# Attention and mixture-of-experts layer on one core: the order of VectorE in the local attention, the place of the expert loads and splits, and the rope's buffers are changed

## The chip, the cores and the metric

One Trainium2 chip, one of its cores. The metric is the device time of one execution in microseconds; lower is better. The engines are named as the profile names them: PE (TensorE, matmul; PEld its weight loads), DVE (VectorE), ACT (ScalarE), POOL (GpSimd), SP (SyncE, which here only issues DMAs).

## The reference

```python
x  = L0_attn_x                       # (2, 1024, 256), float32
xn = layernorm(x)
return x + attention(xn) + experts(xn)
```

Attention: 16 query heads on 4 key-value heads. Each score is the sum of a "semantic" product (32 wide) and a "geometric" product (32 wide, with rope), scaled, times exp(logit_scale) of the head. The first 896 keys are pooled to 14 block means of 64 keys each; the last 128 keys are kept as they are, so there are 142 keys. A query sees the keys whose position is not after its own. Softmax, weighted values, output projection.

Experts: 16 experts, the top 4 of a softmax over 16 logits per token, weights normalised; each expert is silu(x G) * (x U) and a down projection, 256 to 224 to 256. The reference computes all experts and picks; the kernel computes only the chosen ones.

## The kernel before, in words

The five engines run programs of their own, written out by hand and tied by semaphores. The order in which each engine's instructions are written is the order in which it runs them, so a waiting instruction holds up all behind it. On DVE, `link` makes the engine wait for its own last result (needed when the next instruction reads it).

The work comes in four stages.

1. Layer norm, router, ranking of the tokens by expert, block means of the keys. POOL then writes each token's row to the place of each of its four experts in memory, by indirect DMA (L715): 16 groups of 4, each group waited for (L720-L721) before the next. SP loads experts 0 to 3 early (EARLY = 4).

2. The local part: the last 128 queries of both batches, which see all 142 keys. It has eight units (UNITS: 2 batches x 4 key-value heads). For unit n:
   - PE `l_score` (L1510, two banks; it waits until the exponentials of n-2 have read the banks), DVE `l_largest` (L1177), ACT `l_exp` (L835), DVE `l_probabilities` (reciprocal L1184, L1185, L1187, then semaphore l_p), PE `l_turn` (L1527, waits l_p), ACT `l_keep` (L842), PE `l_value` (L1536, waits for the copy of the values before, l_osb), DVE `l_values` (L1193).
   - PE's loop (L1655-L1661): turn n, score n+2, value n-1, `beside(n)`. DVE's loop (L1241-L1248): probabilities n+1, largest n+2, values n-1, `beside(n)`.
   - `beside` is side work. DVE: at n = 0 `build_values` and `diagonals` (L1142, L1145, L1126; they wait for PE's products of that step), at 2 `keep_tables` (L1205 to L1216), at 3, 4 and 7 `split_low` of an expert's weights (L1197, L1198). PE: at 0 the products for the values, at 1 to 3 `fold_values`, at 1 a spread of the task table, at 5 and 6 `fold_queries`.

3. The block part, `attention` over seven pairs of query tiles t (REMOTE = 7). Each step ropes and projects the queries of t+1 while it scores t and attends t-1. `rope_q` (L1147-L1158) reads the projected queries from a PSUM bank: two sine products to q2, a link, the cosine product in place in the bank, a link, the sum to q1. `probabilities` (L1295-L1306) writes the reciprocals of the sums to PSUM columns and multiplies.
   During this stage SP stores and loads residual tiles (`store_sum` L586, `load_residual` L580) and loads the experts 4 to 15 in the seven lots of LATE = ((4, 5), (6, 7), (8, 9), (10, 11), (12,), (13,), (14, 15)) (`load_late` L591; each expert is three DMAs, L401-L403, of 224 KB each). `load_residual(i)` waits until the store two tiles before has landed; `load_behind` (L618) waits for scores of a pair.
   The weights are used as a high half and a low half. ACT makes the high halves (`split_high`, L817 and L818), in the block part those listed for t in SPLITS (L378), 11 and 12 at the head of stage 4, 13 to 15 in its steps 5 to 7. POOL makes the low halves of experts 4 to 12 (L692, L695): 4 and 5 between its last groups, 6 to 12 in a loop after them. DVE makes those of 0 to 3 and 13 to 15.

4. The experts: 79 tiles of 128 rows, software-pipelined. In `step(j)` (L1716) PE turns the input of tile j+2 (L1723), does gate and up of j+1, turns the activations of j (L1747), does the down projection of j-1: 16 matmul instructions a tile. Gate-up of tile 10 waits until all low halves exist (L1734). ACT copies the result y (L938) to one of four buffers; from the fifth on it waits until the scatter of the buffer's last use has landed. POOL scatters y into the output with an add (L742), and begins only after its low halves, with all residual stores landed (L729-L731). SP may load the first expert inputs when the scores of the last pair are done (L640) and all 16 groups of POOL have landed (L642).

Of the kernel before, what the change touches and what calls it, by code (L numbers as in the profile page):

```python
# [32 lines left out]
ALU = mybir.AluOpType  # L33
# [3 lines left out]
P = 128  # L37
# [55 lines left out]
def build(nc, x, wq_sem, wk_sem, wq_geo, wk_geo, wv, wo, logit_scale, router_w, expert_bias, gate, up, down,  # L93
# [9 lines left out]
    with ctx:  # L103
# [72 lines left out]
        bd_g = wat.take("bd_g", [P, HKV, NB, NBLK, G])  # L176
        pr = [wat.take(f"pr{u}", [P, HK]) for u in range(NB)]
        smax = [wat.take(f"smax{u}", [P, H]) for u in range(NB)]
        ssum = wat.take("ssum", [P, NB, H])

        wl = r_loop[0]
        q2 = wl.take("q2", [P, H * DS])
# [192 lines left out]
        FOLD_BANKS = (4, 4, 4, 0)  # L375
        STARTS_BANK = 1
        HIGH_AT = {0: 0, 1: 1, 5: 2}
        SPLITS = ((), (4, 5), (), (6, 7), (8, 9), (10,), ())  # L378
        HEAD = (11, 12)
        SENT = 11  # L380
        BETWEEN = (4, 5)
# [31 lines left out]
        def turned_bank(u, t):  # L413

            return bank[u + 6 if t.last else u]
# [138 lines left out]
        def _(sp):  # L554
# [25 lines left out]
            def load_residual(i):  # L580
                for u in range(NB):
                    if 0 < i < REMOTE - 1:
                        sp.wait_ge(c_stored[u], i * DMA)
                    sp.dma_start(residual(u, i)[:, :], rows(x_rows, u * TB + i)).then_inc(lx_in if i == REMOTE - 1 else xr_in[i % 2][u], DMA)

            def store_sum(i):  # L586
                for u in range(NB):
                    sp.wait_ge(c_out[u], i + 2)
                    sp.dma_start(rows(out_rows, u * TB + i), residual(u, i)[:, :]).then_inc(c_stored[u], DMA)

            def load_late(i):  # L591
                for k in LATE[i]:
                    load_expert(sp, k, w_late[i])
# [18 lines left out]
            sp.wait_ge(tables_ready, 1)  # L612
            for s in range(TRASH):
                sp.wait_ge(scattered[s], DMA)
            load_residual(1)
            load_late(0)
            load_residual(REMOTE - 1)
            def load_behind(n, t):  # L618

                for u in range(NB):  # L620
                    sp.wait_ge(c_s[u], t)
                load_late(n)

            for i in range(REMOTE - 3):
                store_sum(i)
                load_residual(i + 2)
                if i < 3:
                    load_late(i + 1)
                else:
                    load_behind(4, 2)  # L630
            store_sum(REMOTE - 3)
            load_behind(5, 4)

            def load_task(j, s):
                tile = sp.value_load(td_i[0:1, ds(j, 1)], min_val=0, max_val=N * K // P - 1)
# [310 lines left out]
        def _(dve):  # L946
# [197 lines left out]
                                        pmask.rearrange("p (g n h) -> p g n h", g=1, n=1).to_broadcast([P, HKV, NB * NBLK, 2]), ALU.mult)  # L1144
                nc.vector.tensor_copy(vb[:, :, FOLD - NB:FOLD], rep[:, :, NB * NBLK:XF]).then_inc(vb_built, 1)  # L1145

            def rope_q(raw_bank, u, t, done):  # L1147

                raw = raw_bank[:, :].rearrange("p (g h d) -> p g h d", g=H, h=2)
                t2 = q2[:, :].rearrange("p (g h d) -> p g h d", g=H, h=2)  # L1150
                co = cos[:, ds(t * RH, RH)].rearrange("p (o d) -> p o d", o=1).to_broadcast([P, 2 * H, RH])
                for half in range(2):
                    sn = sin[:, ds(t * DS + half * RH, RH)].rearrange("p (o d) -> p o d", o=1).to_broadcast([P, H, RH])
                    last = nc.vector.tensor_tensor(t2[:, :, half, :], raw[:, :, 1 - half, :], sn, ALU.mult)
                link(last)
                by_half = raw_bank[:, :].rearrange("p (g d) -> p g d", d=RH)
                link(nc.vector.tensor_tensor(by_half, by_half, co, ALU.mult))
                nc.vector.tensor_tensor(q1[u][:, :], raw_bank[:, :], q2[:, :], ALU.add).then_inc(done, 1)  # L1158

            def over_keys(v, n=H, k=NBLK):  # L1160
                return v.rearrange("p (h o) -> p h o", o=1).to_broadcast([P, n, k])
# [1 line left out]
            for u in range(NB):  # L1163
                dve.wait_ge(l_q, u + 1)
                if u:
                    dve.wait_ge(l_rope, u)
                rope_q(bank[L_Q[u]], u, REMOTE, l_rope)
            bound_tasks()

            def l_largest(n):  # L1170
# [66 lines left out]

            l_largest(0)
            l_largest(1)
            l_probabilities(0)  # L1240
            for n in range(UNITS):  # L1241
                if n + 1 < UNITS:
                    l_probabilities(n + 1)
                if n + 2 < UNITS:
                    l_largest(n + 2)
                if n:
                    l_values(n - 1)
                beside(n)  # L1248
# [20 lines left out]
            def rope(u, t):  # L1269

                dve.wait_ge(c_q[u], t.count(1))
                if not t.first:
                    dve.wait_ge(c_qt[u], t.count(0))
                if u or not t.first:
                    dve.wait_ge(c_rope[1 - u], t.count(u))
                rope_q(bank[2 + u], u, t.number, c_rope[u])

            def shifted(u, t):

# [15 lines left out]
            def probabilities(t):  # L1295
                dve.wait_ge(c_sum, 2 * t.number + 2)
                if t.first:

                    link(nc.vector.tensor_scalar(ssum[:, :, :], ssum[:, :, :], more[:, 0:1], None, ALU.add))
                srec = [turned_bank(u, t)[:, 0:H] for u in range(NB)]  # L1300
                for u in range(NB):
                    last = nc.vector.reciprocal(srec[u], ssum[:, u, :])
                last.then_inc(c_rec, 1)
                dve.wait_ge(c_rec, t.count(1))
                for u in range(NB):
                    nc.vector.tensor_tensor(by_key(pr[u], t), by_key(pr[u], t), over_heads(srec[u], t), ALU.mult).then_inc(c_p[u], 1)  # L1306

            def attended(u, t):

# [513 lines left out]
```

## Time and profile before

| what | us |
|---|---|
| median of 3 runs | 394.54 |
| lowest and highest | 391.06, 396.1 |
| the profiled execution | 391.06 |
| its span, first to last instruction | 389.3 |
| PE busy | 348.6 (90%) |
| DVE busy | 238.0 (61%) |
| POOL busy | 230.4 (59%) |
| ACT busy | 183.3 (47%) |
| mean granted clock of TensorE | 0.974 |

The busy times are sums over the span and overlap each other. The span leaves out what lies before the first and behind the last instruction, here 1.8 us. All rows further down are of this one execution, in microseconds from the start of its span unless marked ns.

### The profile page before, as it was taken

How to read it: one execution, taken by the hardware profiler on the slowest of the kernel's cores; microseconds unless marked ns; L12 is line 12 of the kernel's file. 1: busy time of each engine (PE TensorE's matmuls, PEld its weight loads, DVE VectorE, ACT ScalarE, POOL GpSimd, SP SyncE). 2: the span in 40 equal slices, each digit the busy share in tenths (PEclk: the TensorE clock that was granted, in tenths of full speed). 3: DMA queues.
4: the chain of work that ended last, by engine and by line, in shares of the span. 5: the costliest groups of instructions: out<-in, count | busy, mean ns of one | idle time of the engine just before them, and what ended most of it. 6: DMA issues, size and time to landing. Idle time of an engine off the chain costs nothing.

```text
span 389.3 us, 8245 instructions
## 1 busy us (share of the span) xinstructions
PE 348.6 (90%) x2103; PEld 283.9 (73%) x2104; DVE 238.0 (61%) x769; ACT 183.3 (47%) x533; POOL 230.4 (59%) x207
## 2 busy tenths in 40 slices
PE   0498999798979999998957999999999999999991
PEld 0393466555756767767947999999999999999881
DVE  3889694687568588864527555555555555555550
ACT  1541325968113236445544555555555555555550
POOL 0510466466554474669986566666666666666664
PEclk9999999999999899998987999999999999999996
DMA  8993112123147477873776567776666766676544
GB/s 254 363 317 90 55 70 82 69 94 133 66 143 215 139 227 246 252 230 103 210 127 94 85 113 109 112 110 106 114 114 106 114 108 108 108 110 109 71 49 54
DMA packets 50094, 52.33 MB, mean 134 GB/s; under 512 B 5632, under 2 KB 47120, under 8 KB 50072
## 3 DMA queue, kind: packets, MB, share of 16 engines
q0 software_dynamic: 14640, 19.34, 30.3%
q1 hardware_dynamic: 35432, 32.73, 29.3%
q8 instruction: 10, 0.16, 0.2%
q14 instruction: 12, 0.10, 0.1%
HBM read 30.14 MB, written 21.91 MB: 134 GB/s over the span
## 4 chain that ended last, share of the span: by engine, by line
PE 77%; DVE 10%; DMA 4%; ACT 4%; issue 2%; SPq 1%; POOLq 1%; DVEq 0%; POOL 0%; ACTq 0%
PE bank L1367 65%; PE bank L1747 4%; PE bank L1723 4%; DMA out_rows<-y,idx 2%; PE bank L1494 2%; DMA x_all<-in_L_attn_x 2%; ACT x_all L764 1%; DVE lneg L1177 1%; DVE lex L1187 1%; ACT lex L835 1%; DVE logit_left L1032 1%; DVE wgu_lo L1197 1%; PE bank L1379 1%; SPq L561 1%; PE bank L1626 1%
## 5 line engine op out<-in xcount | busy, mean ns | idle before, releaser
L742 POOL DMA_INDIRECT out_rows<-y,idx x79 | 124.0, 1569 | 65.7 <-ACT y L938 37.1
L715 POOL DMA_INDIRECT xn_by_expert<-x_all,slot_i x64 | 64.8, 1013 | 55.6 <-DMA xn_by_expert<-x_all,slot_i 34.1
L1367 PE MATMUL bank<-wgu_hi,xh 128*128 x158 | 65.9, 417 | 6.6 <-DVE xl L1339 4.5
L1347 DVE SCALAR_TENSOR_TENSOR act<-bank,xg,sg 128x224 f32<-128x224 f32 x79 | 35.6, 451 | 55.1 <-ACT sg L925 55.1
L1367 PE MATMUL bank<-wgu_lo,xh 128*128 x158 | 59.2, 375 | 0.0
L1367 PE MATMUL bank<-wgu_hi,xl 128*128 x158 | 58.6, 371 | 0.0
L925 ACT ACTIVATE sg<-bank 128x224 f32<-128x224 f32 x79 | 28.3, 358 | 61.7 <-PE bank L1367 61.7
L1339 DVE TENSOR_TENSOR xl<-bank,xh 128x256 fp32r<-128x256 f32 x79 | 33.5, 424 | 33.5 <-ACT xh L916 33.5
L1367 PE MATMUL bank<-wdn_hi,ah 112*128 x158 | 51.6, 327 | 0.6 <-issue 0.5
L1367 PE MATMUL bank<-wdn_hi,al 112*128 x158 | 44.8, 284 | 0.0
L938 ACT COPY y<-bank 128x256 f32<-128x256 f32 x79 | 29.5, 373 | 32.4 <-PE bank L1367 27.6
L1367 PE MATMUL bank<-wdn_lo,ah 112*128 x158 | 44.5, 282 | 0.0
L1367 PEld LDWEIGHTS bank<-wgu_hi,xh 128*128 128x128 f32 x158 | 30.3, 192 | 9.0 <-issue 7.0
L1355 DVE TENSOR_TENSOR al<-bank,ah 112x256 fp32r<-112x256 f32 x79 | 32.8, 415 | 0.5 <-ACT ah L929 0.5
L1367 PEld LDWEIGHTS bank<-wgu_hi,xl 128*128 128x128 f32 x158 | 30.4, 192 | 2.7
L1723 PE MATMUL bank<-const_k,xg 128*128 128x128 f32 x158 | 30.8, 276 | 1.7 <-DMA xg<-xn_by_expert 1.7
L1367 PEld LDWEIGHTS bank<-wgu_lo,xh 128*128 128x128 f32 x158 | 30.6, 194 | 1.2
L916 ACT CAST xh<-bank 128x256 fp32r<-128x256 f32 x79 | 29.9, 378 | 3.3 <-PE bank L1723 3.0
L1367 PEld LDWEIGHTS bank<-wdn_hi,ah 112*128 112x128 f32 x158 | 30.2, 191 | 1.2 <-issue 1.0
L1367 PE MATMUL bank<-wqg,xT 128*128 128x512 f32 x64 | 30.6, 603 | 0.0
L1747 PE MATMUL bank<-const_k,act 128*112 128x128 f32 x158 | 30.4, 274 | 0.0
L1367 PEld LDWEIGHTS bank<-wdn_lo,ah 112*128 112x128 f32 x158 | 30.4, 192 | 0.0
(240 smaller groups left out, 653.2 us busy)
## 6 DMA issues: line engine op xcount, KB each, us to landing
xg<-xn_by_expert SPq DMA_DIRECT2D x79, 129.0 KB, 2.5
wgu<-in_L_ffn_gate_proj SPq DMA_DIRECT2D x16, 224.0 KB, 4.1
wgu<-in_L_ffn_up_proj SPq DMA_DIRECT2D x16, 224.0 KB, 4.8
wdn<-in_L_ffn_down_proj SPq DMA_DIRECT2D x16, 224.0 KB, 5.3
x_all<-in_L_attn_x SPq DMA_DIRECT2D x8, 256.0 KB, 4.7
xr<-in_L_attn_x SPq DMA_DIRECT2D x14, 128.0 KB, 2.4
out_rows<-xr SPq DMA_DIRECT2D x14, 128.0 KB, 2.5
out_rows<-y,idx POOLq DMA_INDIRECT x79, 3.8
```

Of the source, the lines that this page charges most:

```text
L715: gp.indirect_dma_start(xs_d, bass.IndirectOffsetOnAxis(slot_i[:, z, r:r + 1], 0), x_all[:, z, :], None).then_inc(xs_in[p], DMA)
L742: gp.indirect_dma_start(out_rows, bass.IndirectOffsetOnAxis(idx[r % RING][:, 0:1], 0), ysb[r % 4][:, :], None, compute_op=ALU.add).then_in ...
L916: nc.scalar.copy(xh[t.par][:, :, :], bank[t.par][:, 0:D].rearrange("p (c n) -> p c n", c=DC)).then_inc(xh_ready, 1)
L925: nc.scalar.activation(sg[t.par][:, :], bank[2 + t.par][:, 0:I], ACT.Silu).then_inc(sg_ready, 1)
L938: nc.scalar.copy(ysb[t.place][:, :], bank[6 + t.par][:, 0:D]).then_inc(y_ready, 1)
L1339: nc.vector.tensor_tensor(xl[t.par][:, :, :], bank[t.par][:, 0:D].rearrange("p (c n) -> p c n", c=DC), xh[t.par][:, :, :].bitcast(F32), AL ...
L1347: nc.vector.scalar_tensor_tensor(av[t.par][:, :], bank[2 + t.par][:, I:2 * I], xg[t.slot][:, D + 1:D + 2], sg[t.par][:, :], ALU.mult, ALU. ...
L1355: nc.vector.tensor_tensor(al[t.par][:, :, :], bank[4 + t.par][0:IH, 0:2 * P].rearrange("p (c n) -> p c n", c=2), ah[t.par][:, :, :].bitcas ...
L1367: return nc.tensor.matmul(o, lhsT, rhs, start=start, stop=stop)
L1494: last = nc.tensor.transpose(o[:, g * P:(g + 1) * P], q1[u][:, g * P:(g + 1) * P], ident)
L1723: last = nc.tensor.transpose(bank[t.par][:, c * P:(c + 1) * P], xg[t.slot][:, c * P:(c + 1) * P], ident)
L1747: last = nc.tensor.transpose(bank[4 + t.par][0:IH, c * P:(c + 1) * P], av[t.par][:, c * IH:(c + 1) * IH], ident)
```

## The change

- DVE's local loop: step n makes the probabilities of n, not of n+1, so that those of n+1 follow the largest scores of n+2, the values of n-1 and the side work of n.
- Rope: the cosine product is written first, to q1 in SBUF; the two sine products follow, then one link and a sum of q1 and q2. The reciprocals of the sums go to a new SBUF tile srec, in one instruction for both batches.
- ACT's high halves of experts 6 to 10 move one step of the block part earlier (SPLITS).
- SP: the lots 0 to 3 of LATE (experts 4 to 11) are issued in one run, lot 0 ahead of the load of residual 1 and lots 1 to 3 behind it, all ahead of residual 6 and of the first store. Lot 4 (expert 12) comes after store 1 instead of after store 3, lot 5 (expert 13) before store 4 instead of behind it.

```diff
@@ -176,7 +176,7 @@
-        ssum = wat.take("ssum", [P, NB, H])
+        ssum, srec = (wat.take(n, [P, NB, H]) for n in ("ssum", "srec"))
@@ -375,7 +375,7 @@
-        SPLITS = ((), (4, 5), (), (6, 7), (8, 9), (10,), ())
+        SPLITS = ((), (4, 5), (6, 7), (8, 9), (10,), (), ())
@@ -612,8 +612,11 @@
             for s in range(TRASH):
                 sp.wait_ge(scattered[s], DMA)
+            load_late(0)
             load_residual(1)
-            load_late(0)
+            load_late(1)
+            load_late(2)
+            load_late(3)
             load_residual(REMOTE - 1)
...
             for i in range(REMOTE - 3):
                 store_sum(i)
                 load_residual(i + 2)
-                if i < 3:
-                    load_late(i + 1)
-                else:
+                if i == 1:
                     load_behind(4, 2)
+            load_behind(5, 4)
             store_sum(REMOTE - 3)
-            load_behind(5, 4)
@@ -1144,18 +1145,19 @@
-            def rope_q(raw_bank, u, t, done):
+            def rope_q(raw_bank, u, t):
...
+                nc.vector.tensor_tensor(q1[u][:, :].rearrange("p (g d) -> p g d", d=RH), raw_bank[:, :].rearrange("p (g d) -> p g d", d=RH), co, ALU.mult)
                 for half in range(2):
                     sn = sin[:, ds(t * DS + half * RH, RH)].rearrange("p (o d) -> p o d", o=1).to_broadcast([P, H, RH])
                     last = nc.vector.tensor_tensor(t2[:, :, half, :], raw[:, :, 1 - half, :], sn, ALU.mult)
-                link(last)
-                by_half = raw_bank[:, :].rearrange("p (g d) -> p g d", d=RH)
-                link(nc.vector.tensor_tensor(by_half, by_half, co, ALU.mult))
-                nc.vector.tensor_tensor(q1[u][:, :], raw_bank[:, :], q2[:, :], ALU.add).then_inc(done, 1)
+                return last
+
+            def rope_sum(u, done):
+                nc.vector.tensor_tensor(q1[u][:, :], q1[u][:, :], q2[:, :], ALU.add).then_inc(done, 1)
@@ -1164,7 +1166,8 @@
-                rope_q(bank[L_Q[u]], u, REMOTE, l_rope)
+                link(rope_q(bank[L_Q[u]], u, REMOTE))
+                rope_sum(u, l_rope)
@@ -1237,10 +1240,8 @@
             l_largest(0)
             l_largest(1)
-            l_probabilities(0)
             for n in range(UNITS):
-                if n + 1 < UNITS:
-                    l_probabilities(n + 1)
+                l_probabilities(n)
                 if n + 2 < UNITS:
                     l_largest(n + 2)
@@ -1273,7 +1274,8 @@
-                rope_q(bank[2 + u], u, t.number, c_rope[u])
+                link(rope_q(bank[2 + u], u, t.number))
+                rope_sum(u, c_rope[u])
@@ -1297,13 +1299,10 @@
-                srec = [turned_bank(u, t)[:, 0:H] for u in range(NB)]
-                for u in range(NB):
-                    last = nc.vector.reciprocal(srec[u], ssum[:, u, :])
-                last.then_inc(c_rec, 1)
+                nc.vector.reciprocal(srec[:, :, :], ssum[:, :, :]).then_inc(c_rec, 1)
                 dve.wait_ge(c_rec, t.count(1))
                 for u in range(NB):
-                    nc.vector.tensor_tensor(by_key(pr[u], t), by_key(pr[u], t), over_heads(srec[u], t), ALU.mult).then_inc(c_p[u], 1)
+                    nc.vector.tensor_tensor(by_key(pr[u], t), by_key(pr[u], t), over_heads(srec[:, u, :], t), ALU.mult).then_inc(c_p[u], 1)
```

## Rows read from the trace of the kernel before

**Rows 1.** The page, chain that ended last, shares of the span by engine

```profile
PE 77%; DVE 10%; DMA 4%; ACT 4%; issue 2%; SPq 1%; POOLq 1%; DVEq 0%; POOL 0%; ACTq 0%
```

**Rows 2.** Table of stretches: from:to, length, busy us of each engine (instructions), clock, DMA share, GB/s

```profile
66.00:80.00 14.00, 11.95 (x82) 7.45 (x78) 8.42 (x25) 11.05 (x40) 7.94 (x10) 1.00 0.20 74
130.00:134.00 4.00, 4.00 (x13) 2.96 (x14) 1.32 (x6) 1.17 (x2) 2.44 (x4) 0.57 0.60 189
134.00:172.60 38.60, 38.60 (x228) 28.96 (x227) 30.83 (x83) 16.36 (x41) 22.85 (x23) 1.00 0.81 248
198.80:212.80 14.00, 7.42 (x34) 6.62 (x33) 8.77 (x19) 8.33 (x20) 10.79 (x7) 0.76 0.74 107
212.80:378.00 165.20, 164.74 (x1098) 153.45 (x1099) 90.07 (x273) 86.99 (x273) 105.30 (x69) 1.00 0.66 103
```

**Rows 3.** Timeline of PE, local loop: start, length, instruction [idle before, releaser]

```profile
70.22 0.66 PE L1527 MATMUL bank<-const_k,lex 128*128 128x128 f32 x4 [2.06 <-DVE lex L1187]
...
72.21 1.97 PE L1367 MATMUL bank<-x_fold,wv_rep 128*128 128x30 f32 x16
74.02 0.64 PE L1527 MATMUL bank<-const_k,lex 128*128 128x128 f32 x4
...
75.98 0.65 PE L1367 MATMUL bank<-lpT,vloc 128*64 128x256 f32 x4
...
78.31 0.60 PE L1527 MATMUL bank<-const_k,lex 128*128 128x128 f32 x4
...
95.76 0.66 PE L1527 MATMUL bank<-const_k,lex 128*128 128x128 f32 x4 [0.50 <-DVE lex L1187]
```

**Rows 4.** Timeline of DVE, local loop

```profile
74.22 0.39 DVE L1142 TENSOR_TENSOR vb<-bank,const_c 128x224 f32<-128x224 f32 x1 [1.08 <-PE bank L1367]
...
75.15 0.16 DVE L1184 RECIPROCAL lrec<-lsum 128x4 f32<-128x4 f32 x1
...
81.42 0.22 DVE L1205 TENSOR_SCALAR task_expert<-bank 1x79 int32<-1x79 f32 x1
...
84.11 0.17 DVE L1184 RECIPROCAL lrec<-lsum 128x4 f32<-128x4 f32 x1
...
86.10 1.09 DVE L1197 TENSOR_TENSOR wgu_lo<-wgu,wgu_hi 128x896 fp32r<-128x896 f32 x1
...
87.70 0.17 DVE L1184 RECIPROCAL lrec<-lsum 128x4 f32<-128x4 f32 x1
```

**Rows 5.** DVE timeline (a rope), PE's waits 102 to 122 us (total, times, longest)

```profile
111.16 0.75 DVE L1154 TENSOR_TENSOR q<-bank,const_k 128x256 f32<-128x256 f32 x2
111.94 0.70 DVE L1157 TENSOR_TENSOR bank<-bank,const_k 128x512 f32<-128x512 f32 x1
112.68 0.69 DVE L1158 TENSOR_TENSOR q<-bank,q 128x512 f32<-128x512 f32 x1
...
PE bank L1494 <- DVE q L1158: 2.0, 2, 1.4
```

**Rows 6.** Timeline of POOL: indirect writes, low halves, first scatter

```profile
86.59 1.46 POOL L715 DMA_INDIRECT xn_by_expert<-x_all,slot_i  x1 [0.31 <-issue]
...
120.56 0.97 POOL L715 DMA_INDIRECT xn_by_expert<-x_all,slot_i  x1 [5.21 <-DMA xn_by_expert<-x_all,slot_i]
...
172.99 2.08 POOL L692 TENSOR_TENSOR wgu_lo<-wgu,wgu_hi  x1 [2.01 <-DMA xn_by_expert<-x_all,slot_i]
...
196.30 1.62 POOL L742 DMA_INDIRECT out_rows<-y,idx  x1
```

**Rows 7.** Timeline of ACT (fifth result), and PE's waits from 176 to 216 us

```profile
200.61 0.37 ACT L938 COPY y<-bank 128x256 f32<-128x256 f32 x1 [4.85 <-DMA out_rows<-y,idx]
...
PE bank L1367 <- DVE wdn_lo L1198: 2.1, 1, 2.1
```

**Rows 8.** SP timeline (one issue); DMA view from 116 to 122 us

```profile
115.05 0.47 SPq L403 DMA_DIRECT2D wdn<-in_L_ffn_down_proj  x1
...
DMA packets 1733, 1.62 MB, mean 270 GB/s; under 512 B 132, under 2 KB 1701, under 8 KB 1733
```

## The prediction

> **What bounds the kernel now.** Read the chain of waits first: by engine it is PE for 77% of the span, DVE for 10% [rows 1]. So an edit pays where PE is not fed. Then read the table of stretches for where that is [rows 2]: from 134.0 to 172.6 us (the block attention) PE is busy for all of 38.60 us, and from 212.8 to 378.0 us (the expert loop) for 164.74 of 165.20. In 198.8 to 212.8 it is busy for only 7.42 of 14.00 us, at a mean granted clock of 0.76. Last, the timelines of PE, DVE and POOL show what feeds PE in the two loose stretches: the loop over the eight local units (66 to 102 us) and the start of the experts.
>
> In the local loop PE turns the probabilities of unit n, makes the scores of unit n+2, the output of unit n-1, and some side work. Turn 0 starts at 70.22, turn 7 at 95.76: 25.5 us [rows 3]. DVE is ahead of it, because it makes the probabilities of n+1 before it touches the largest scores of n+2 and its side work.
>
> At the start of the experts POOL is late. Its 16 groups of indirect writes have landed at 172.99, then it makes low halves of the weights, and its first scatter starts at 196.30, 23.3 us later [rows 6]. Four result buffers are full by then: ACT sits 4.85 us until that scatter has landed and writes the fifth at 200.61; PE stands still behind it, and later 2.1 us for the third DVE split [rows 7]. One tile takes 165.2 us / (1098 / 16 matmuls) = 2.41 us; the 34 matmuls between 198.8 and 212.8 are worth 34 / 16 x 2.41 = 5.1 us [rows 2], so 14.0 - 5.1 = 8.9 us are lost there.
>
> **The change, part by part.** *Order of DVE in the local loop (the term that decides).* Each step now issues the probabilities of n only, so those of n+1 come behind the largest scores of n+2, the copy of n-1's values and the side work of step n. But PE makes the scores of n+2 only after turn n, and turn n wants the probabilities of n. Behind the waiting DVE instruction stand the side work and the next probabilities, and PE's next turn waits for these. Durations, start to start: turn and scores 75.98 - 74.02 = 1.96 [rows 3]; probabilities, largest scores and values 86.10 - 84.11 = 1.99; side work 0.93 in step 0 (74.22 to 75.15), 2.69 in step 2 (81.42 to 84.11), 1.60 in steps 3 and 4 (86.10 to 87.70) [rows 4]. With about 0.15 for semaphores, a turn-to-turn step costs 1.96 + 1.99 + 0.15 = 4.1 plus side work, unless PE's own work is longer:
> step 0: turn, scores and PE's products for the values up to 74.02 as before (72.21 is their start), then DVE's side work and about 1 us for probabilities: turn 1 at 76.15 instead of 74.02, so 5.9;
> step 1: PE's own, 1.96 + 2.33 (75.98 to 78.31) = 4.3;
> step 2: 4.1 + 2.7 = 6.8; steps 3 and 4: 5.7 each; step 5: 4.15; step 6, without new scores: 2.5.
> The sum is 35.1 (rounded) against 25.5: **+9.6 us**. It gives PE gaps of 2 to 3.4 us where there were none or 0.5. Lower end: if only steps 2 and 4 stall, +6.5; upper end +10.5, if each handover costs 0.1 more.
>
> *Rope.* Before, a second linked step wrote the cosine product into the bank; now it goes to SBUF ahead of the sine pair, and one link falls. The step from 111.16 to 112.68 was 1.52 to the last sum [rows 5]; three products in a row, overlapped by about 0.09 each, are 0.70 + 0.75 - 0.09 = 1.36 and a link. That is -0.13 a rope. Sixteen ropes give DVE 2 us, but in the dense attention PE covers them; on the path are the two for which PE waited (2.0 us in two waits [rows 5]): -0.3 us. The same for one reciprocal over 32 columns instead of two over 16, and for SBUF in place of PSUM: between -0.3 and +0.3, I take 0, since PE is busy throughout.
>
> *High halves one attention step earlier.* ACT is no bound there; 0, between 0 and +0.5. What it removes are ACT's waits for experts 8 to 10, which PE never felt.
>
> *Loads.* SP now issues experts 4 to 11 in one go, moves residual 6 and the first store behind them, experts 12 and 13 earlier. The first store has nothing to do until its tile is ready, 18 us after the loads start, so SP is not late. The cost is on POOL: with the loads of two experts in flight one group of indirect writes held POOL for 5.21 us, against 2.01 for the last one [rows 6]: 3 us. Eight experts of 3 x 224 KB are 5.4 MB, 20 us at 270 GB/s, but SP issues them in 24 x 0.5 = 12 us [rows 8]. So one group will meet a backlog of 7 to 8 us, the one before it 3; but the later groups, which met two experts each time, now run clear (three more meetings, at up to 3 us each). Some 12 us saved with the first, 10 to 11 paid, 2 for experts 12 and 13: I take +1 for the end of POOL's groups, from -3 to +8. It only matters if POOL's first scatter then comes too late.
>
> The Trainium skill (SBUF — State Buffer, "SBUF: two separate sides") says that VectorE and GpSimd lock each other out of a shared port pair when a VectorE operation has two SBUF inputs. The trace agrees: beside DVE's split of the weights (86.10 to 87.70 [rows 4]) an indirect write took 1.46 us against 0.97 [rows 6]. By that rule the new rope sum, SBUF plus SBUF where it was PSUM plus SBUF, blocks POOL: some 6 of 14 sums meet a write, up to 0.5 us each, an estimate of 3 us on POOL's end; that alone stays below the point of rival B.
>
> *What the later PE does at the experts.* Attention ends near 182, not 172.6. POOL's groups (end 173 to 181) no longer set its start, and the first scatter still comes 23.3 us behind them, at 196 to 204, for the low halves wait for no PE work that is late enough: the last high halves, experts 11 and 12, move with PE to about 190, and they are POOL's last two (3.3 us each, 189.5 and 192.8). The fifth result was due at 200.61 - 4.85 = 195.8 [rows 7], now at 195.8 + 9.3 = 205.1; the first scatter lands at 200.6 + 0 to 5. So that stall and its half-clock time go. What stays is the DVE splits in three consecutive tiles: 3 x 1.60 + 2 x 1.31 (90.07 us / 68.6 tiles [rows 2]) = 7.4 us from the first split's start to the third's end, while the gate of tile 10 is due about 1.8 tiles, 4.3 us, after that start: 3.1 us lost. Loads of experts 14 and 15 now run beside the first scatters: 0 to 4 us more. I take 3.6 in place of the old 8.9, ends 3.1 and 8.9: **-5.3 us**.
>
> *Clock.* At 130 to 134 us PE was granted 0.57 of its clock, which cost 4.0 x 0.43 = 1.7 us [rows 2]. The local loop had 1.00 in spite of a gap of 2.06 us [rows 2, 3]. With four gaps of 1.4 to 3.4 us I take +1, from 0 to 3.5. The Trainium skill (TensorE: Matmul & The Clock Gate, Part 1) says that an idle PE is dropped to 1.2 GHz and has to earn 2.4 back; that speaks against this change and would make it rival C. Row 198.8 to 212.8, 0.76 after a long stall, agrees; the local loop's first gap does not.
>
> **Sum**: +9.6 - 0.3 - 5.3 + 1.0 = +5.0. Against the profiled execution, 391.06 us (span 389.3 and 1.8 around it), that is 396.1. This execution is the fastest of three; on the median, 394.54, it is 399.5, which I give.
>
> **Rivals.** *A: the stall pays for all, not slower than before.* Place: tiles 4 to 10. If POOL's scatters land before the fifth result and the splits cost 3.1 or less, and the half-clock stretch at 130 us (1.7 us) does not come back, the sum is 9.3 - 5.8 - 1.7 = +1.8; with a loop loss below 7.8 it is 0 or less: 394. It decides at that loop loss. For it: only PE's order bounds the recurrence. Against: DVE and PE work are both known to 0.1 us, so 9.6 is firm.
> *B: POOL stays late.* If eight experts' loads hold up the writes until 181 or later, the first scatter lands after 208 and the stall comes back behind the later start: 9.3 + 0 to 4, 404 to 408. It decides at 5 us of delay. For it: 3 us lost to two experts' loads. Against: the groups after the burst run clear.
> *C: the clock.* Two half-clock stretches in the loop: +3.5 rather than +1, 402.0.
> *D: the loop order hides.* If the new order let DVE work ahead (the largest scores no longer stand behind a wait for the exponentials) it would gain at most PE's gaps of the loop's 14 us from 66 to 80, 2 us [rows 2], and the loss at the experts' start would stay: 392. Against: the scores of n+2 do not exist yet at that place.
>
> **How the numbers follow.** Forecast 0.57, A 0.12, B 0.18, C 0.10, D 0.03. Range 392.5 to 407.0: the sum's ends (3.1 us less in the splits' term to B's middle) and 2 us for the scatter of executions. A measurement of this kernel tells about 2%, 7.9 us, from no change. Over +7.9 (402.4) lie B and a third of C with the forecast's tail: slower 0.24; faster 0.02; within 2% 0.74.
>
> **What would show it.** Right: turn 0 to turn 7 of about 35 us with PE waiting for the probabilities before turns 1, 3, 4, 5; DVE waiting about 2.1 us for the scores before every largest-score pair; attention ending near 182; no ACT wait of over 2 us for a scatter at the fifth result. Wrong: a loop under 30 us; POOL's groups ending after 181; a granted clock below 1.00 between 75 and 105 us for more than 5 us; or a start of the experts earlier than 180.

## The result, and the profile after

The changed kernel takes 415.21 us in the median of four runs (413.63 to 416.35), against 394.37 us for the kernel before beside it (four runs, 391.06 to 396.1). The ratio is 1.0536, with a 95% interval from 1.0455 to 1.0619. Now and then an execution comes out over 1.5% above the fastest of its kernel, at a lower granted clock: such slow ones are left out of every ratio, and of the times given for e2 and e4 below. The forecast of 399.5 us and its range up to 407.0 were too low. The profiled execution of after took 415.77 us, with a span of 414.0; the one of before had a span of 389.3, so the profiles show 24.7 us, some 4 more than the medians: the profiled execution of before is the fastest of its runs.

Four marks on PE divide the span into five stretches: turn 0 and turn 7 of the local loop, the first expert product, and the gate of tile 10, behind which PE is fed almost without a gap. The two last ones of before, from its timeline of PE, are

```profile
177.63 0.58 PE L1367 MATMUL bank<-wgu_hi,xh 128*128 x1
...
212.79 0.47 PE L1367 MATMUL bank<-wgu_hi,xh 128*128 x1 [2.09 <-DVE wdn_lo L1198]
```

and after, turns (L1526) and expert products (L1366) in its timeline of PE:

```profile
70.86 0.66 PE L1526 MATMUL bank<-const_k,lex 128*128 128x128 f32 x4 [2.06 <-DVE lex L1190]
76.80 1.11 PE L1526 MATMUL bank<-const_k,lex 128*128 128x128 f32 x4 [1.99 <-DVE lex L1190]
82.58 0.60 PE L1526 MATMUL bank<-const_k,lex 128*128 128x128 f32 x4
89.48 0.66 PE L1526 MATMUL bank<-const_k,lex 128*128 128x128 f32 x4 [3.46 <-DVE lex L1190]
96.78 0.66 PE L1526 MATMUL bank<-const_k,lex 128*128 128x128 f32 x4 [1.36 <-DVE lex L1190]
102.63 0.66 PE L1526 MATMUL bank<-const_k,lex 128*128 128x128 f32 x4 [3.21 <-DVE lex L1190]
...
110.64 0.66 PE L1526 MATMUL bank<-const_k,lex 128*128 128x128 f32 x4 [0.39 <-DVE lex L1190]
...
186.16 0.69 PE L1625 MATMUL bank<-const_k,pr 128*128 128x128 f32 x2 [8.24 <-DVE pr L1305]
...
206.08 0.60 PE L1366 MATMUL bank<-wgu_hi,xh 128*128 x1
...
235.90 0.47 PE L1366 MATMUL bank<-wgu_hi,xh 128*128 x1 [2.49 <-DVE wdn_lo L1201]
```

Subtract mark from mark, with turns 0 and 7 of before at 70.22 and 95.76 [rows 3]:

| stretch | before | after | difference |
|---|---|---|---|
| start to turn 0 | 70.2 | 70.9 | +0.6 |
| turn 0 to turn 7 | 25.5 | 39.8 | +14.2 |
| turn 7 to first expert product | 81.9 | 95.4 | +13.6 |
| first expert product to gate of tile 10 | 35.2 | 29.8 | -5.3 |
| gate of tile 10 to the end | 176.5 | 178.1 | +1.6 |

The second row was foreseen as +9.6 and 1 for the clock, the fourth as -5.3. The third, the dense and the block attention, was foreseen as nothing. The one PE wait of 8.24 us in the fence above lies there. Who held it stands in DVE's timeline of after:

```profile
142.81 1.53 DVE L1160 TENSOR_TENSOR q<-q,q 128x512 f32<-128x512 f32 x1
...
154.17 1.71 DVE L1160 TENSOR_TENSOR q<-q,q 128x512 f32<-128x512 f32 x1
...
171.41 2.49 DVE L1160 TENSOR_TENSOR q<-q,q 128x512 f32<-128x512 f32 x1
...
176.25 11.15 DVE L1305 TENSOR_TENSOR pr<-pr,srec 128x160 f32<-128x160 f32 x2
```

Two products of the probabilities with their reciprocals, 128x160, took 11.15 us together. The view of that line has 302 ns in its median and 9849 ns in its longest instruction: the first of the two, from 176.25 to 186.10. The rope sum `q<-q,q` takes 0.69 us alone, and up to 2.49 here. Both lines have two inputs in SBUF since the change; before, one of the two was in PSUM. The last products of before stood under the same loop of POOL, which began at 172.99 [rows 6], and took 0.68 us together in DVE's timeline:

```profile
176.26 0.68 DVE L1306 TENSOR_TENSOR pr<-pr,bank 128x224 f32<-128x224 f32 x2
```

What ran beside the long ones of after is in POOL's timeline of after, which answers to [rows 6] too:

```profile
174.08 2.09 POOL L693 TENSOR_TENSOR wgu_lo<-wgu,wgu_hi  x1 [0.74 <-DMA xn_by_expert<-x_all,slot_i]
176.11 1.28 POOL L696 TENSOR_TENSOR wdn_lo<-wdn,wdn_hi  x1
177.34 2.08 POOL L693 TENSOR_TENSOR wgu_lo<-wgu,wgu_hi  x1
179.37 1.28 POOL L696 TENSOR_TENSOR wdn_lo<-wdn,wdn_hi  x1
...
185.86 1.37 POOL L696 TENSOR_TENSOR wdn_lo<-wdn,wdn_hi  x1
187.19 2.16 POOL L693 TENSOR_TENSOR wgu_lo<-wgu,wgu_hi  x1
...
208.49 2.08 POOL L693 TENSOR_TENSOR wgu_lo<-wgu,wgu_hi  x1 [17.47 <-ACT wdn_hi L819]
...
216.25 1.62 POOL L743 DMA_INDIRECT out_rows<-y,idx  x1 [1.10 <-ACT y L939]
```

POOL makes low halves back to back all through DVE's 11 us, in 2.08 and 1.28 us each as before, but for the one at 185.86 with 1.37. The loop begins at 174.08, as foreseen (172.99 before). Then POOL itself waits 17.47 us for the high halves of expert 11, since ACT stands behind PE, PE behind DVE.

The table of stretches of after (columns as in [rows 2]) and, last, the page's chain by engine, which answers to [rows 1]:

```profile
76.00:80.00 4.00, 3.20 (x14) 2.19 (x14) 0.75 (x2) 1.94 (x3) 1.94 (x4) 0.57 0.09 33
89.00:95.00 6.00, 5.52 (x22) 2.73 (x22) 2.48 (x5) 2.50 (x10) 3.06 (x5) 0.72 0.24 86
103.00:108.00 5.00, 4.99 (x26) 2.90 (x25) 2.14 (x6) 3.49 (x11) 4.00 (x5) 0.66 0.66 186
...
181.00:186.00 5.00, 0.00 (x0) 0.00 (x0) 5.00 (x1) 0.00 (x0) 5.00 (x4) 0.63 0.10 33
186.00:191.00 5.00, 4.23 (x8) 1.98 (x9) 4.49 (x8) 1.19 (x5) 5.00 (x3) 0.50 0.00 0
```

```profile
PE 72%; DVE 12%; issue 5%; DMA 4%; SPq 3%; ACT 3%; POOLq 1%; DVEq 0%
```

Three stretches of the local loop run at a reduced clock. From 181 to 186 us DVE has one instruction and is busy for all 5.00 us with it, PE has none; then PE's clock is at half for five more. In the chain PE has lost five points of the span; "issue" (no releaser that the profile shows) has gained three, DVE and SP's issues two each.

With that the third row of the table adds up. PE's waits for the products are 8.9 us (8.24 and 0.62); its waits for rope sums grew from 2.0 to 3.1 us; behind the long wait the granted clock is 0.50 from 186 to 191 us and 0.92 from 191 to 201, worth 2.5 and 0.8. Together 13.3 of the 13.6 us.

### The profile page after: what moved, and what is told of

Its sections match the earlier page's. It is cut to its first block, busy times and chain, and to the rows that moved or that the text cites. A ratio compares the mean times of both kernels' runs of the same rounds, so it can differ in the third digit from the quotient of the medians.

```text
span 414.0 us, 8237 instructions
## 1 busy us (share of the span) xinstructions
PE 357.0 (86%) x2103; PEld 287.1 (69%) x2104; DVE 251.3 (61%) x762; ACT 184.1 (44%) x533; POOL 232.3 (56%) x207
## 4 chain that ended last, share of the span: by engine, by line
PE 72%; DVE 12%; issue 5%; DMA 4%; SPq 3%; ACT 3%; POOLq 1%; DVEq 0%
PE bank L1366 60%; PE bank L1722 4%; PE bank L1746 4%; DMA xg<-xn_by_expert 2%; DMA x_all<-in_L_attn_x 1%; PE bank L1493 1%; PE bank L1526 1%; DVE wgu_lo L1200 1%; DVE lex L1190 1%; ACT x_all L765 1%; DMA out_rows<-y,idx 1%; SPq L636 1%; DVE q L1160 1%; DVE q L1153 1%; DVE q L1156 1%
## 5 line engine op out<-in xcount | busy, mean ns | idle before, releaser
L1366 PE MATMUL bank<-wgu_hi,xh 128*128 x158 | 65.3, 413 | 2.6 <-DVE wdn_lo L1201 2.5
L1366 PE MATMUL bank<-wgu_lo,xh 128*128 x158 | 58.9, 373 | 0.0
L1366 PE MATMUL bank<-wgu_hi,xl 128*128 x158 | 58.3, 369 | 0.0
L1366 PE MATMUL bank<-wdn_hi,ah 112*128 x158 | 51.6, 327 | 0.6 <-issue 0.5
L1366 PE MATMUL bank<-wdn_hi,al 112*128 x158 | 44.7, 283 | 0.0
L1366 PE MATMUL bank<-wdn_lo,ah 112*128 x158 | 44.5, 281 | 0.0
L1366 PEld LDWEIGHTS bank<-wgu_hi,xh 128*128 128x128 f32 x158 | 30.0, 190 | 5.1 <-issue 3.1
L1366 PE MATMUL bank<-wqg,xT 128*128 128x512 f32 x64 | 32.5, 635 | 0.0
L1366 PEld LDWEIGHTS bank<-wgu_hi,xl 128*128 128x128 f32 x158 | 30.1, 190 | 2.7
L1366 PEld LDWEIGHTS bank<-wgu_lo,xh 128*128 128x128 f32 x158 | 30.3, 192 | 1.2
L1366 PEld LDWEIGHTS bank<-wdn_hi,ah 112*128 112x128 f32 x158 | 30.1, 191 | 1.2 <-issue 1.1
L1366 PEld LDWEIGHTS bank<-wdn_lo,ah 112*128 112x128 f32 x158 | 30.3, 192 | 0.0
```

Source lines behind the costliest of these rows:

```text
L1366: return nc.tensor.matmul(o, lhsT, rhs, start=start, stop=stop)
```

## The experiments

The reasons to tell apart were these. *Lock*: DVE instructions with two SBUF inputs are held while POOL makes low halves. *Clock*: the gaps of the new loop order drop TensorE's clock. *Loads*: the earlier burst of loads slows the block part. *Loop*: the new order costs its +9.6 and no more. The parts first, each alone or left out.

**e1: only the loop order.** Before, with

```
-            l_probabilities(0)
             for n in range(UNITS):
-                if n + 1 < UNITS:
-                    l_probabilities(n + 1)
+                l_probabilities(n)
```

> The kernel before with the new order of the local loop alone; rope, reciprocals, loads and splits as before. Theory 1 (two costs: the local loop is 14 us longer, and DVE operations with two SBUF inputs are held up while POOL makes low halves): the loop from turn 0 to turn 7 takes 39 to 40 us as in the changed kernel, but no DVE product or rope sum takes over 1 us, and after the earlier loss at the experts' start is given back (5 us) the time is 9 to 11 us over before: 403 to 406. Theory 2 (the late loop alone makes the 10 us stall of the block part, through POOL or the loads): the stall is there too and the time is 412 to 416.

Measured: 404.16 us (399.27 to 405.24) against 395.08; ratio 1.0233, from 1.0181 to 1.0284. Turn 0 at 70.85, turn 7 at 109.52: 38.7 us, +13.1. The first expert product is at 189.74, the gate of tile 10 at 219.39: 29.7 us, -5.5. No DVE instruction in the block part is longer than 1.1 us. So the order costs 9.1, where the terms of the prediction for it make 9.6 - 5.3 + 1.0 = 5.3. The experts' start is as foreseen, the loop with its clock is not: 13.1 for 9.6 + 1.0. e7 below parts the two.

**e2: all but the loop order.** After, with the old order of the loop:

```
+            l_probabilities(0)
             for n in range(UNITS):
-                l_probabilities(n)
+                if n + 1 < UNITS:
+                    l_probabilities(n + 1)
```

> The changed kernel with the old order of the local loop alone. Theory 1: the loop takes 25.5 us again, the block part ends near 173, just as POOL's loop of low halves begins, so few DVE operations meet it and the time falls to 392 to 398. Theory 2, and any theory in which the 10 us stall comes from the buffers or loads whatever the lateness: 402 to 406.

Measured: 398.74 and 398.94 us in the two executions that count, 3.8 over the 395.08 of before (the other two took 407.53 and 407.78; two are too few for an interval). The expectation of 392 to 398 was missed by 0.8. The lock had moved to the last products, for which PE waited 7.2 us:

```profile
178.32 10.32 DVE L1307 TENSOR_TENSOR pr<-pr,srec 128x224 f32<-128x224 f32 x2
```

**e3: the SBUF operands back in PSUM.** After, with

```
-                nc.vector.reciprocal(srec[:, :, :], ssum[:, :, :]).then_inc(c_rec, 1)
+                srec = [turned_bank(u, t)[:, 0:H] for u in range(NB)]
+                for u in range(NB):
+                    last = nc.vector.reciprocal(srec[u], ssum[:, u, :])
+                last.then_inc(c_rec, 1)
```

and the cosine product of the rope in the bank again.

> The changed kernel with rope and reciprocals in PSUM as before; the new loop order, loads and splits stay. Theory 1: the 9.8 us product and the rope sums of 1.7 and 2.5 us are gone, 9 to 12 us off the changed kernel: 403 to 406. Theory 2 (loads or splits make the stall): 413 to 416, and another instruction shows the long duration.

Measured: 403.35 us (400.96 to 405.51); ratio 1.0234, from 1.0163 to 1.0306. No DVE instruction from 98 to 205 us is longer than 1.1 us. The SBUF operands thus cost 415.21 - 403.35 = 11.9 us within the change.

**e4: only the SBUF operands.** Before, with rope and reciprocals as in the change:

```
-                srec = [turned_bank(u, t)[:, 0:H] for u in range(NB)]
...
+                nc.vector.reciprocal(srec[:, :, :], ssum[:, :, :]).then_inc(c_rec, 1)
...
-                rope_q(bank[2 + u], u, t.number, c_rope[u])
+                link(rope_q(bank[2 + u], u, t.number))
+                rope_sum(u, c_rope[u])
```

> The kernel before with the rope sum and the products in SBUF alone. Theory 1: the block part ends before POOL's loop begins, and only single low halves of POOL (two between its groups) can hold a DVE operation, for at most 2 us each, under PE's dense work: within 3 us of before, 392 to 397. A theory in which two SBUF inputs cost DVE time whatever POOL does: 5 us or more over before.

Measured: 398.77 us in the median of the seven executions that count (397.23 to 402.12; 400.41 with the other three); ratio 1.0099, from 1.006 to 1.0138, which is 3.9 us. The expectation of 392 to 397 was missed here too, and its rival, 5 us or more, was not reached. Timeline of DVE, and of PE behind it:

```profile
185.38 7.85 DVE L1306 TENSOR_TENSOR pr<-pr,srec 128x224 f32<-128x224 f32 x2
```

```profile
191.91 0.69 PE L1626 MATMUL bank<-const_k,pr 128*128 128x128 f32 x2 [5.30 <-DVE pr L1306]
```

I had taken it that before's DVE would be through when POOL's closing loop begins; its last products are not.

Why 3.9 us alone and 11.9 in the change? The marks of e4 are 72.51, 98.50, 193.83 and 223.58. Turn 7 to the first expert product takes 95.3 us, 13.5 more than before and as much as in after. (The profiled execution is the longest of the seven. 6.0 us are PE's waits for the last products; 5.2 are the granted clock, 0.53 from 171 to 182 us, whose cause no run shows.) But the first expert product to the gate of tile 10 takes 29.8 us, 5.4 less than before: a block part that ends later finds the first scatter in time (in e4 that scatter, at 204.57, had itself waited 1.54 us for a result). The same was given back by the loop order alone (e1, 5.5) and by e2 (5.6), and with order and operands together it is still 5.3. It can be had once. So 9.1 (e1) + 3.9 (e4) + 5.4 = 18.4 of the 20.8 us. That the later DVE also meets more of POOL's loop may make the rest; it isn't shown by itself.

The next four ask which instruction is caught, what the clock took, and what a free DVE would be worth.

**e5 and e6: one of the two operands back in PSUM.** e5 takes the reciprocals back, with the diff of e3; e6 the cosine product of the rope:

```
+                link(last)
+                by_half = raw_bank[:, :].rearrange("p (g d) -> p g d", d=RH)
+                link(nc.vector.tensor_tensor(by_half, by_half, co, ALU.mult))
+                nc.vector.tensor_tensor(q1[u][:, :], raw_bank[:, :], q2[:, :], ALU.add).then_inc(done, 1)
```

> The changed kernel with the reciprocals in PSUM again; the rope sum keeps its two SBUF inputs. Theory 1 (any DVE operation with two SBUF inputs waits while POOL runs its low halves back to back): the products are short again, but a rope sum takes their place behind POOL's loop; one L1160 of 5 us or more, and most of the changed kernel's time stays: 409 to 415. A rival in which the product alone is slow (its broadcast of srec, its tile): 403 to 405.

> The changed kernel with the rope's cosine product in PSUM again; the products keep two SBUF inputs. Theory 1: no rope sum over 1 us, the long product of about 10 us stays; 1 to 3 us off the changed kernel: 411 to 415.

Measured: e5 412.69 us (ratio 1.043, from 1.0383 to 1.0477), e6 412.61 (1.0459, from 1.0406 to 1.0513). Each half gives back some 2.5 us of the 11.9, hardly more than the executions scatter (after has 413.63 to 416.35, e5 410.82 to 415.57). In e5 the rope sum is caught in place of the product, in e6 the product again. So neither the product's shape nor its tile is the cause. DVE timelines of e5, then e6:

```profile
180.27 6.03 DVE L1160 TENSOR_TENSOR q<-q,q 128x512 f32<-128x512 f32 x1
```

```profile
171.94 11.66 DVE L1302 TENSOR_TENSOR pr<-pr,srec 128x160 f32<-128x160 f32 x2
```

**e7: PE kept busy in the loop.** After, with idle products ahead of turns 1, 3, 4 and 5, into the bank that the turn overwrites:

```
+                for _ in range({1: 14, 3: 24, 4: 8, 5: 24}.get(n, 0)):
+                    mm(bank[6][:, 0:2 * P], ident_b[:, :], ..., True, True)
+                pe.wait_ge(l_p, n + 1)
```

> The changed kernel with idle products on PE ahead of turns 1, 3, 4 and 5 of the local loop (14, 24, 8 and 24 of 256 columns, written to a bank that is overwritten next; they leave the results as they are). If PE's idle gaps are what takes the clock to half in the loop (three such stretches, 4 us): granted clock 1.00 from 70 to 110 us, turn 0 to turn 7 in 35 to 36.5 us instead of 39.8, and 3 to 5 us off the changed kernel, unless the later stages wait for POOL anyway. If the clock falls for another reason: the loop stays at 39 us or grows.

Measured: 413.03 us (410.03 to 414.82); ratio 1.0429, from 1.0368 to 1.049. Table of stretches and timeline of PE of e7:

```profile
76.00:80.00 4.00, 3.54 (x28) 2.29 (x26) 1.80 (x7) 1.94 (x3) 1.65 (x3) 1.00 0.18 66
89.00:95.00 6.00, 5.48 (x34) 2.84 (x32) 3.65 (x8) 2.62 (x10) 3.26 (x4) 1.00 0.30 108
103.00:108.00 5.00, 3.90 (x30) 2.88 (x32) 2.75 (x9) 2.77 (x11) 2.52 (x3) 1.00 0.44 145
```

```profile
71.41 0.66 PE L1528 MATMUL bank<-const_k,lex 128*128 128x128 f32 x4 [2.07 <-DVE lex L1190]
...
77.35 0.66 PE L1528 MATMUL bank<-const_k,lex 128*128 128x128 f32 x4 [0.46 <-issue]
...
107.37 0.63 PE L1528 MATMUL bank<-const_k,lex 128*128 128x128 f32 x4 [0.48 <-issue]
```

The same three stretches have the full clock, and turn 0 to turn 7 takes 36.0 us instead of 39.8. So 3.8 us of the loop were the clock, and the rest is the order: 36.0 - 25.5 = 10.4. The total fell by 2.2, which is within the scatter, not by 3.8: turn 7 came 3.3 us sooner, the first expert product only 1.6 (204.49). Part of that is the clock once more: 0.79 from 122 to 130 us and 0.61 from 152 to 156, 3.2 us, against one such stretch of 1.6 in after (144 to 148, 0.60). And DVE was caught again:

```profile
180.37 8.27 DVE L1160 TENSOR_TENSOR q<-q,q 128x512 f32<-128x512 f32 x1
```

Put the catches side by side. Each loop start is from POOL's timeline, each end is start plus duration of the one long instruction (where a row joins two products, of the one that was held):

| kernel | closing loop starts | caught | its end | end after loop start |
|---|---|---|---|---|
| after | 174.08 | product | 186.10 | 12.0 |
| e2 | 176.42 | product | 188.64 | 12.2 |
| e4 | 179.77 | product | 191.86 | 12.1 |
| e5 | 173.41 | rope sum | 186.30 | 12.9 |
| e6 | 171.52 | product | 183.60 | 12.1 |
| e7 | 175.78 | rope sum | 188.64 | 12.9 |

The long instructions asked at any time from 2.2 to 6.9 us after the loop's start, and all came out 12.0 to 12.9 us after it: POOL sets the end. In each case that is just behind the first half of the fourth pair of low halves (in after that half ends at 185.92). An instruction that asks earlier, during the loop's very first low half, gets in behind that one: e5 has a rope sum at 174.74 of 1.32 us, e7 one at 176.75 of 1.66. This fits that half a cure (e5, e6) or an earlier DVE (e7) gave so little. What lets DVE in at these places and not between stays open.

**e8: POOL holds its closing loop until the last probabilities are stored.**

```
+            for u in range(NB):
+                gp.wait_ge(c_p[u], REMOTE)
             with gp.Fori(BETWEEN[-1] + 1, IN_LOOP) as e:
```

> The changed kernel with one wait more: POOL starts its loop of low halves when the last products of the block part are made. Theory 1: every product and rope sum behind 172 us takes under 1 us, the block part ends near 190 instead of 201, and POOL's first scatter comes at 216 or later, so that the time is given back at the fifth result: 408 to 418 in all. If the product is slow for a reason of its own: it still takes about 10 us.

Measured: 412.49 us (two runs, 410.05 to 414.93); ratio 1.044, from 1.0355 to 1.0526. The view of the product's line in e8 (min/median/max ns), where the instructions are those of after and only POOL's work beside them is away:

```profile
L1308 DVE TENSOR_TENSOR pr<-pr,srec x14: 188/288/392, 139.0 to 191.5; 128x32 f32<-128x32 f32 x2, 128x64 f32<-128x64 f32 x2, 128x96 f32<-128x96 f32 x2, 128x128 f32<-128x128 f32 x2
```

Its longest is 0.39 us where after had 9.85. Together with e3 this shows the cause: the long products need both two SBUF inputs on DVE and POOL's loop beside them. In time the hold gives almost nothing. PE, POOL and ACT timelines of e8:

```profile
192.57 0.53 PE L1369 MATMUL bank<-wgu_hi,xh 128*128 x1
...
222.23 0.73 PE L1369 MATMUL bank<-wgu_hi,xh 128*128 x1 [8.66 <-DVE xl L1341]
```

```profile
192.38 2.11 POOL L693 TENSOR_TENSOR wgu_lo<-wgu,wgu_hi  x1 [20.45 <-DVE pr L1308]
...
215.73 1.62 POOL L746 DMA_INDIRECT out_rows<-y,idx  x1
```

```profile
219.51 0.37 ACT L942 COPY y<-bank 128x256 f32<-128x256 f32 x1 [8.82 <-DMA out_rows<-y,idx]
```

The experts start 13.5 us sooner (192.57 for 206.08), but POOL's first scatter is where it was (215.73 for 216.25), so the fifth result waits 8.82 us for it. PE's wait is put down to DVE's `xl`, which stood behind ACT. That is the wait of [rows 7] again.

**e9: only the loads, and the slots of ACT's high halves** (SPLITS; the expectation calls them low halves).

```
+            load_late(0)
             load_residual(1)
-            load_late(0)
+            load_late(1)
+            load_late(2)
+            load_late(3)
...
```

> The kernel before with only the moved loads and the moved low-half slots: the late group's loads are issued at once ahead of the block part and three experts' low halves one stage earlier or later, as in the change; loop order and SBUF operands stay as before. Theory (loads cost next to nothing, as the prediction said with its +1 on POOL's groups): time within 3 us of before, 392 to 398 us, POOL's first low half of the closing loop at 172 to 176 us of the span, the up projection's transfers land in 6 us or more where before they took 4.8. Rival (part of the change's 20 us is the fuller queue itself, which slows the indirect writes and so the scatters): 399 to 405 us and the closing loop of low halves starts at 177 us or later.

Measured: 395.15 us (390.86 to 396.5, ten runs) against 394.7; ratio 0.9988, from 0.9948 to 1.0028. The loop starts at 175.89, the up projection lands in 7.4 us. The median landing of an up projection was 4.8 us before. The loads cost nothing that can be told.

**e10 and e11: two or three low halves behind the first scatters.** Before, with

```
-            with gp.Fori(BETWEEN[-1] + 1, IN_LOOP) as e:
+            with gp.Fori(BETWEEN[-1] + 1, IN_LOOP - LATER) as e:
...
+            for r in range(RING):
+                scatter(r, r, r + 1)
+                if r < LATER:
+                    for part in range(2):
+                        split_low(IN_LOOP - LATER + r, part)
```

> The kernel before, with POOL's low halves of the last two experts put behind its first and second scatter instead of ahead of all scatters; nothing else. Before, ACT's fifth result waited 4.85 us for the first scatter, which started at 196.30 us when POOL's low halves were done. Theory (the first scatter is what the experts' start waits for): the first scatter starts near 190 us, that wait is gone or under 1 us, a later one of up to 3 us may come at the sixth or seventh result, total 388 to 392 us. Rival (another wait ends just behind it, the low halves of DVE or the landing of the gathered rows): 393 to 396 us, with a PE idle time of 3 us or more between 195 and 212 us that is released by something other than a scatter.

> The same with the last three experts' low halves, one behind each of the first three scatters. Theory: the first scatter starts near 187 us and the third near 197 us; 387 to 392 us, equal to the version with two or up to 2 us below it. Rival (low halves come too late for the experts that need them, or POOL's scatters fall behind by the inserted 3.3 us each): 393 us or more.

Measured: e10 394.03 us against 394.7 (ratio 1.0, from 0.9956 to 1.0044), e11 393.7 (0.9964, from 0.9925 to 1.0004). In e10 the first scatter starts at 189.84 and the 4.85 us wait is gone, but the rival held:

```profile
209.93 0.74 PE L1372 MATMUL bank<-wgu_hi,xh 128*128 x1 [4.95 <-DVE wdn_lo L1203]
```

PE stands 4.95 us for a DVE low half of an expert, one wait behind the one removed. In e11 the first scatter starts at 190.01, and PE stands 3.93 us for DVE's `xl`, while DVE's first low half waits 3.8 us for POOL's last one. Neither version is shown to beat the kernel before.

**e12: the hold of e8 with three low halves behind the scatters.** After, with the lines of e8 and e10 together and

```
-        IN_LOOP = 13
+        IN_LOOP, LATER = 13, 3
```

> The changed kernel with POOL's closing loop of low halves held back until the last probabilities are stored, as in the run with the hold, and three of its seven experts put behind the first three scatters. The hold alone brought the first expert product forward by 13.5 us (192.57 against 206.08) but the first scatter stayed at 215.73, ACT waited 8.8 us for it and the time came out at 412.5. Theory (the lock costs about 13 us of the block part, and with the hold the first scatter gives it back): first scatter near 206 us, the wait of 8.8 us falls below 5, total 403 to 409 us. Rival (something else than the scatter holds the experts' start): the wait in the experts' start stays at 8 us or more in sum and the total at 411 to 414 us.

Measured: 409.02 us (405.12 to 410.03, four runs) against 394.7; ratio 1.0352, from 1.0307 to 1.0398. The first scatter is at 203.30, the longest wait for one 2.3 us, but PE waits 6.78 us: DVE's own low half stands 6.6 us for POOL's. At the edge of what was expected, and 3.5 under e8: the first scatter took part of the 13.5 us, POOL's low halves the rest. The version free of the lock, e3, is 5.7 us better than this one.

## Why the prediction was wrong, step by step

*Loop order, +9.6: right.* At full clock (e7) the steps are 5.9, 4.3, 6.9, 5.9, 5.8, 4.3 and 2.8 us, where 5.9, 4.3, 6.8, 5.7, 5.7, 4.15 and 2.5 were worked out; +10.4 in all. PE waits before turns 1, 3, 4 and 5, as said, and DVE for the scores before each largest value, 2.4 us in the mean of eight waits (before had 4.6 us in four). The waits of after, 66 to 113 us (total, times, longest):

```profile
DVE lneg L1180 <- PE bank L1366: 19.4, 8, 3.6
...
PE bank L1526 <- DVE lex L1190: 12.5, 6, 3.5
```

The rule used, that a recurrence costs the way around it (PE scores, DVE largest, the side work before the next probabilities), can be relied on. Rival D, that the order hides, fell, and with a loop loss of 10.4 rival A too, which wanted less than 7.8.

*SBUF for PSUM, "between -0.3 and +0.3, I take 0, since PE is busy throughout": the step that failed.* It is 11.9 us in the change (after less e3) and 3.9 alone (e4), where the experts' start hides some 5 of it. The price was taken from the duration of the instruction alone, and the cover was never asked for its end: PE waits for each of these products, so a cover holds only as long as DVE is less late than PE is busy, and behind a long wait the clock is low as well (3.3 us here). [rows 6] showed what would lie beside them, seven pairs of low halves in a row from 172.99, and that the attention would end nine us behind that start (182 against 173) was in the prediction itself. The first expert product came at 206.08; e3, without the SBUF operands, had it at 190.95. The two facts were not put together.

The Trainium skill (SBUF — State Buffer, "SBUF: two separate sides") says that a VectorE operation with two SBUF inputs and a GpSimd operation that reads SBUF exclude each other, and that the later one blocks. The prediction asked it only what POOL would lose. The trace shows the other side: POOL kept its 2.08 and 1.28 us, and DVE stood. By the page's words (held for the whole instruction of the other) an estimate is one low half, 2.1 us, for a product; the measured 9.85 us lie across several. So the trace agrees with the page in kind, and a price worked out from it would still have been too small.

*Rope, -0.3: right where POOL is away.* The three products and the sum go from 123.24 to 125.31 us in after, and the step that was 1.52 [rows 5] is 1.38:

```profile
123.24 0.68 DVE L1153 TENSOR_TENSOR q<-bank,const_k 128x512 f32<-128x512 f32 x1
123.84 0.74 DVE L1156 TENSOR_TENSOR q<-bank,const_k 128x256 f32<-128x256 f32 x2
124.62 0.69 DVE L1160 TENSOR_TENSOR q<-q,q 128x512 f32<-128x512 f32 x1
```

*Loads, +1 for the end of POOL's groups: right* (174.08 for 172.99; e9 the same time as before). SP's issues ran from 0.47 us [rows 8] up to 1.41 in the full queue, and no one waited for them. Rival B, POOL late by the loads, fell; POOL's first scatter was late in the end, but for another reason, the high halves that stood behind the lock.

*Experts' start, -5.3: right*, -5.3 in after and -5.5 in e1. The fifth result has no wait, and PE waits 2.49 us for the third DVE low half, [rows 7] having 2.1.

*Clock, +1.0 with +3.5 as its end: right in kind, too small.* Three stretches at 0.57 to 0.72 took 3.8 us (after less e7). The half-clock stretch at 130 us (0.57, 1.7 us [rows 2]) moved: 130 to 144 us has 1.00, and 144 to 148 has 0.60, 1.6 us. The Trainium skill (TensorE: Matmul & The Clock Gate, Part 1) says that an idle PE is dropped to 1.2 GHz. The loop agrees: idle products in the gaps brought 1.00 back. The single first gap of 2.06 us in [rows 3] had misled the prediction into about a quarter of the price. Rival C's mechanism was there, its 402.0 was not the total.

With the measured sizes, 10.4 - 0.3 - 5.3 + 3.8 is +8.6, near e1's +9.1 and e3's +8.3; the lock adds 11.9, and 20.8 was measured. One of the prediction's own signs of being wrong came: a clock below 1.00 between 75 and 105 us for more than 5 us. None of its signs, and none of its rivals, looked at DVE under POOL's loop.

## What to carry to other kernels

Before moving an operand from PSUM to SBUF on DVE, look at POOL's timeline for the same stretch, in the kernel as it will be: beside a row of POOL tensor operations, a DVE instruction with two SBUF inputs can stand for the better part of the row, small as it is. "PE is busy throughout" is a cover only for a lag shorter than PE's queue; ask what ends the lag. And when a wait is removed (e8, e10), name the next one behind it first: here the first scatter, DVE's low halves and POOL's low halves stood one behind the other. The same holds for a saving: two changes that each end the same wait give it back once, so their costs alone (9.1 and 3.9) do not add up to the cost of both.

## What the runs showed of the hardware that was not expected

- A DVE instruction of 0.3 us was held for 9.85 us by a row of POOL tensor operations that each took 1.3 to 2.1 us, one behind the other without idle time in the record. In six kernels such an instruction came free 12.0 to 12.9 us after the row began, wherever in the first 7 us it had asked, but for those that asked during the row's first operation.
- In that row POOL loses little: one low half of 1.72 us for 1.28 here and there. Single scatters beside DVE's own splits of weights lost more, 2.40 for 1.55 us in e10.
- With one of the two inputs in PSUM the products stayed short under the same row (0.68 us for two, in before).
- In the new loop gaps of 1.99 to 3.46 us went with a granted clock of 0.57 to 0.72 in the stretches behind them; filled with idle products, 1.00. Stretches of 0.57 to 0.61 came in the block part too, at 130 us in before, 144 in after and 152 in e7.
- The loads of eight experts in one go raised the landing of an up projection from 4.8 to 7.4 us (e9) and cost no time.
